# Attention scores in 32-row tiles on a packed key tile, with the exponentials' scale in a register

## The chip, the core and the metric

The kernel runs on one core of one Trainium2 chip. The metric is device time in microseconds, the median of several executions. TensorE (PE) multiplies, VectorE (DVE) reduces and normalises, ScalarE (ACT) computes exponentials and copies, GpSimd (POOL) and SyncE (SP) set things up and issue transfers.

## What is computed

Six sub-layers work on one sequence of 2048 rows of 128 numbers: expert feed-forward, attention, expert feed-forward, ternary feed-forward, attention, ternary feed-forward, each on the layer-normalised rows and added to the residual. The change touches the two attention layers (16 heads of 8 numbers each, causal):

```python
q, k, v = (split_heads(y) for y in (x @ wq, x @ wk, x @ wv))    # 16 heads x 8
scores = where(causal, einsum('bhqd,bhkd->bhqk', q, k), -inf)
attn = softmax(scores / sqrt(8))
x = x + einsum('bhqk,bhkd->bhqd', attn, v) (@ wo + bo in the first)
```

## The kernel before, in words

**Queries and keys as rows.** Each number of q and k is split into float16 parts, so that a head takes TERMS x 8 = 24 rows, plus 8 rows for the negative row maximum (two parts, MAX_UNIT on the key's side) and zeros: 32 rows, a "slot". Four heads (G = 4) make 128 rows, a group g; there are NG = 4 groups. The rows go through DRAM (`slot_dram`) and come back by SP's and POOL's loads (`load_k_rows`, L1084 to L1088, called at L1382 to L1383 and L1397 to L1399; q's at L1394). `q_slots` [128, 4, 2048] holds the four heads of a group together. `k_slots` [128, 16, 2048] holds each head by itself, at its own 32 rows of 128, and zeros in the other 96, so that a matmul over all 128 rows gives one head's scores. POOL writes these zeros once, at the start of the kernel (L620), and then 32 rows of MAX_UNIT (L622); the same tile is the source of the constant rows that SP stores to DRAM at L380 to L385.

**Steps, quads and units.** A step is a pair (g, c) of a group and a chunk c of 512 queries (CH). Steps are taken with c = 0, 1, 2, 3 for g = 0, 1, and then c = 3, 2, 1, 0 for g = 2, 3 (`STEPS`). A step has two kinds of work.

The *units* find the row maximum: for a block of 128 queries, a head and a chunk of 512 keys, PE computes the scores with queries on the partitions (L1204) into one of three PSUM banks, a ring, and DVE reduces them: `tensor_reduce` at L1314, or, on the diagonal, an instruction that also adds the causal mask (L1320). Successive units have successive heads h = 0 to 3. When a step's units are done, DVE makes the negative maximum (L1368), PE turns it (L1209), DVE splits it (L1341, L1343) and SP writes it into `q_slots` (L1410).

The *quads* do the rest, one for each 128 keys j of a step: `score_tile` (L1155 to L1176) computes the scores of two heads, with keys on the partitions, into two banks (L1164), twice; if the quad is on the diagonal (4 quads of each step), a matmul of all 128 rows with `ident_bf` adds the mask to its first 128 columns (L1171). ACT takes the exponentials of each tile of two heads (L1275). `values` (L1178 to L1189) then multiplies them by `v_aug`, four heads in four column groups of 32 (L1184), in float32, which makes eight matmuls a quad. Diagonal quads have 512, 384, 256 and 128 query columns.

**The order.** PE's program is written out turn by turn: score tile 0 of a quad, some ring items, score tile 1, some, the values of the quad before, the rest. `units_beside_quads` gives each turn its number of units, from their columns and from due times (a step's units are done 3 quads before it begins; the first two steps' units run ahead of all quads). A score tile waits for the exponentials of the tile two before it, a unit for its ring bank, the values for their exponentials.

**The scale.** DVE computes one number per layer (`exp_scale`, L818) at the start, and signals `qk_scaled` at L824. The exponentials read it as an operand, a column of SBUF.

The line numbers are those of the profile.

Of the kernel before, what the change touches and what calls it, by code (L numbers as in the profile page):

```python
# [7 lines left out]
F16 = mybir.dt.float16  # L8
I32 = mybir.dt.int32
# [53 lines left out]
def macaron_layers(nc, x_in, wq, wk, wv, wo, bo, wr, w1, b1, wo2, bo2, gamma, beta,  # L63
# [16 lines left out]
    with stack:  # L80
# [15 lines left out]
        q_slots = sb("q_slots", [P, NG, T], F16)  # L96
        k_slots = sb("k_slots", [P, H, T], F16)
        exp_scale = sb("exp_scale", [P, 2])
# [21 lines left out]

        dve_chain = Chain(sem("dve_own"))

        slot_dram = [nc.dram_tensor(f"{n}_rows", [H, TERMS + 1, DH, T], F16, kind="Internal").ap() for n in ("q", "k")]
# [157 lines left out]
        def expert_layer(first, order, given, norms, next_norms, released=None, following=None):  # L281
# [23 lines left out]
            if first:  # L305
# [15 lines left out]
                def staged(cols, rows=P):  # L321
# [25 lines left out]
                    sem("qk_max_ready"), sem("qk_max_turned"), sem("qk_diag_ready"), sem("qk_max_all"))  # L347
                rest_rows_stored, qk_scaled = sem("rest_rows_stored"), sem("qk_scaled")

# [249 lines left out]
            def _(pool):  # L599
                if first:  # L600
# [18 lines left out]

                    pool.memset(k_slots[:, :, :].rearrange("p h t -> p (h t)").bitcast(I32), 0).then_inc(slots_set, 1)  # L620
                    pool.wait_ge(slots_set, 1)
                    pool.memset(k_slots[0:H * MAX_PARTS, 0, :], MAX_UNIT).then_inc(slots_set, 1)  # L622
# [442 lines left out]
        def attention_layer(proj, layer, projected, given, next_norms, next_given, released):  # L1065
# [15 lines left out]

            def load_k_rows(engine, n, h):  # L1084

                cols = slice(n * CH, (n + 1) * CH)
                return engine.dma_start(k_slots[SLOT * h:SLOT * (h + 1), h::G, cols],
                                        slot_dram[1].rearrange("(g h) i d t -> h (i d) g t", h=G)[h, :, :, cols])  # L1088

# [62 lines left out]
            def _(pe):  # L1152
                def score_tile(q, pr):

                    (g, c), j = q  # L1155
                    n = quad_no[q]
                    off = first_query(q)
                    if j == 0 and pr == 0:
                        pe.wait_ge(negmax_landed[step_no[q[0]] % 4], 16 * MAX_PARTS * (step_no[q[0]] // 4 + 1))
                    tile = 2 * n + pr  # L1160
                    if tile >= 2:
                        pe.wait_ge(exp_done, tile - 1)
                    for par in range(2):
                        last = pe.matmul(psum[:, S_BANKS + 2 * (tile % 2) + par, off:CH],  # L1164
                                         k_slots[:, G * g + 2 * pr + par, j * P:(j + 1) * P],
                                         q_slots[:, g, c * CH + off:(c + 1) * CH],
                                         start=True, stop=q not in diagonal)
                    if q in diagonal:

                        for par in range(2):  # L1170
                            last = pe.matmul(psum[:, S_BANKS + 2 * (tile % 2) + par, off:off + P],  # L1171
                                             ident_bf[:, :], later_keys[:, :], start=False, stop=True)
                    last.then_inc(scores_done, 1)
# [16 lines left out]
                def ring_item(item):  # L1190
# [5 lines left out]
                    if kind == "scores":  # L1196
                        (g, c), i, kc, h = what
                        if (g, i, kc, h) == (0, 0, 0, 0):
                            pe.wait_ge(q_landed[c], 16 if c else 16 * (G + 1))
                            if c:  # L1200
                                pe.wait_ge(k_landed[c - 1], 16 * G)
                        w = CH if kc < c else (i + 1) * P
                        qb = BPC * c + i
                        last = pe.matmul(psum[:, bank, 0:w], q_slots[:, g, qb * P:(qb + 1) * P],  # L1204
                                         k_slots[:, G * g + h, kc * CH:kc * CH + w], start=True, stop=True)
                    elif kind == "max":
# [54 lines left out]
            @blk.scalar  # L1261
            def _(act):
                for n in range(1, NCH):
                    proj.high_parts(act, n)
                for (q, _), (_, _, copy_out, _) in zip(TURNS, PLAN):
                    if q:
                        n = quad_no[q]
                        off = first_query(q)
                        for pr in range(2):
                            tile = 2 * n + pr  # L1270
                            act.wait_ge(scores_done, tile + 1)
                            if tile >= NP:
                                act.wait_ge(pv_done, (tile - NP) // 2 + 1)
                            bank = S_BANKS + 2 * (tile % 2)
                            act.activation(probs[:, tile % NP, :, off:CH], psum[:, bank:bank + 2, off:CH],  # L1275
                                           ACT.Exp, scale=exp_scale[:, layer:layer + 1]).then_inc(exp_done, 1)
                    for s in copy_out:
# [94 lines left out]
            @blk.gpsimd  # L1372
            def _(pool):

                for n in range(1, NCH):
                    pool.wait_ge(parts_stored[n % 2], 16 * 2 * TERMS * (n // 2 + 1))
                    for h in range(G):
                        load_k_rows(pool, proj.order[n], h).then_inc(k_landed[proj.order[n] - 1], 16)

            @blk.sync  # L1380
            def _(sp):
                def slots_of(n):  # L1382
# [5 lines left out]
                    for m in range(2):  # L1388
                        sp.wait_ge(proj.lo_ready, 2 * n + m + 1)
                        for i, r in enumerate((Q_PARTS, K_PARTS)[m]):  # L1390
                            sp.dma_start(slot_dram[m][:, i, :, cols],
                                         proj.parts_of(n, m)[:, r, :]).then_inc(parts_stored[n % 2], 16)
                    sp.wait_ge(parts_stored[n % 2], 16 * 2 * TERMS * (n // 2 + 1))
                    sp.dma_start(q_slots[:, :, cols],  # L1394
                                 slot_dram[0].rearrange("(g h) i d t -> (h i d) g t", h=G)[:, :, cols]
                                 ).then_inc(q_landed[c], 16)
                    if n == 0:  # L1397
                        for h in range(G):
                            load_k_rows(sp, c, h).then_inc(q_landed[c], 16)  # L1399

# [55 lines left out]
```

## Time and profile before

| | us |
|---|---|
| median of 3 runs | 1316.02 (1314.12 to 1316.12) |
| span of the profiled execution | 1311.0 |
| PE matmul busy | 1194.1 |
| DVE busy | 1044.4 |
| ACT busy | 723.5 |
| POOL busy | 66.6 |

The profile is of one execution. Its span goes from its first to its last instruction; its own time outside the span is not recorded, and the medians are of other executions of the same program. The first attention layer's quads run from 202.5 to 640.9 us, the second's from 848.5 to 1277.5. Busy time of an engine is the time in which at least one of its instructions was under way; starts of matmuls are recorded, their ends are modelled.

### The profile page before, as it was taken

The page shows a single profiled execution, that of the slowest core. Times are in us where ns is not written, and L with a number is a line of the kernel's source. Part 1 is how long each engine was busy: PE and PEld are TensorE (multiplying, and loading weights), DVE is VectorE, ACT ScalarE, POOL GpSimd, SP SyncE. Part 2 cuts the span into 40 slices and gives each one's busy share as a digit, 9 for nine tenths or more (in the row PEclk, how much of TensorE's full clock was granted, in tenths as well). Part 3 has the DMA queues.
Part 4 walks back from the last instruction along what each step waited for, and adds up shares of the span by engine and source line. Part 5 has one row for each costly group of instructions (what it writes and reads, how often), then busy time and mean ns, then how long its engine had stood idle before and what let it go on. Part 6 is the DMA issues. An engine that isn't in the chain of part 4 may idle for free.

```text
span 1311.0 us, 21446 instructions
## 1 busy us (share of the span) xinstructions
PE 1194.1 (91%) x7781; PEld 510.1 (39%) x7781; DVE 1044.4 (80%) x3015; ACT 723.5 (55%) x861; POOL 66.6 (5%) x64
## 2 busy tenths in 40 slices
PE   1999958999999999999699979599999999999997
PEld 1455533333333333334455537233333333333336
DVE  8976588999999887875447567799999989878764
ACT  1322115566777777777332224156667777777773
POOL 5111010000000000000101000100000000000000
PEclk9999979999999999999799989799999999999999
DMA  4100142000000000000000000510000000000001
GB/s 147 34 1 1 39 131 58 2 1 2 2 1 1 2 1 2 1 1 2 1 0 1 1 1 25 154 48 2 2 1 2 2 1 1 2 1 2 2 2 33
DMA packets 23510, 23.26 MB, mean 18 GB/s; under 512 B 3134, under 2 KB 21220, under 8 KB 23404
## 3 DMA queue, kind: packets, MB, share of 16 engines
q1 hardware_dynamic: 22252, 18.73, 4.9%
q0 software_dynamic: 1152, 3.15, 0.9%
q8 instruction: 62, 1.02, 0.3%
q14 instruction: 44, 0.36, 0.1%
HBM read 13.20 MB, written 8.39 MB: 16 GB/s over the span
## 4 chain that ended last, share of the span: by engine, by line
PE 70%; DVE 22%; issue 4%; ACT 2%; DMA 1%; SPq 0%; DVEq 0%; ACTq 0%
PE psum L1184 18%; PE psum L1204 17%; PE psum L1164 14%; PE psum L442 9%; DVE part_max L1314 8%; PE psum L466 2%; PE psum L903 2%; PE psum L1171 2%; DVE junk L1320 2%; DVE xn L167 1%; DVE norm_v L150 1%; PE psum L1224 1%; PE psum L918 1%; DVE norm_stats L141 1%; PE psum L427 1%
## 5 line engine op out<-in xcount | busy, mean ns | idle before, releaser
L1275 ACT ACTIVATE hidden<-psum,exp_scale 128x1024 f32<-128x1024 f32 (+3 forms) x640 | 597.7, 984 | 258.9 <-PE psum L1164 137.3
L1314 DVE TENSOR_REDUCE part_max<-psum 128x1 f32<-128x512 f32 x768 | 492.1, 686 | 59.1 <-PE psum L1204 53.9
L1204 PE MATMUL psum<-k_slots,q_slots 128*128 128x512 f16 (+3 forms) x1280 | 401.2, 356 | 34.2 <-DVE part_max L1314 12.2
L1164 PE MATMUL psum<-q_slots,k_slots 128*128 128x512 f16 (+3 forms) x1280 | 330.9, 348 | 6.3 <-ACT hidden L1275 3.5
L1184 PE MATMUL psum<-hidden,v_aug 128*9 128x512 f32 (+3 forms) x2560 | 293.7, 531 | 0.1
L1320 DVE CUSTOM_DVE_ANT_0 junk<-psum,causal_add 128x384 bf16<-128x384 f32 (+3 forms) x512 | 230.6, 488 | 49.0 <-PE psum L1204 45.9
L1204 PEld LDWEIGHTS psum<-k_slots,q_slots 128*128 128x128 f16 x1280 | 114.5, 97 | 361.1 <-DVE part_max L1314 177.5
L442 PE MATMUL psum<-parts,w_parts 128*128 128x512 f16 x768 | 180.4, 387 | 1.9 <-DVE parts L843 1.9
L1164 PEld LDWEIGHTS psum<-q_slots,k_slots 128*128 128x128 f16 x1280 | 118.3, 98 | 97.8 <-ACT hidden L1275 13.9
L442 PEld LDWEIGHTS psum<-parts,w_parts 128*128 128x128 f16 x768 | 73.7, 99 | 83.1 <-issue 6.8
L586 ACT CAST parts<-psum 128x512 f16<-128x512 f32 x64 | 37.2, 588 | 107.2 <-PE psum L427 107.2
L1184 PEld LDWEIGHTS psum<-hidden,v_aug 128*9 128x9 f32 x2560 | 38.0, 88 | 91.6 <-issue 81.0
L1171 PE MATMUL psum<-later_keys,ident_bf 128*128 128x128 bf16 x512 | 69.0, 219 | 0.0
L843 DVE TENSOR_TENSOR parts<-parts 128x1024 f16<-128x1024 f16 x64 | 46.8, 755 | 18.2 <-ACT parts L586 18.2
L1171 PEld LDWEIGHTS psum<-later_keys,ident_bf 128*128 128x128 bf16 x512 | 47.5, 98 | 25.2 <-issue 0.7
L1320 DVE DVE_READ_ACCUMULATOR2_ANT part_max<- 128x1 f32 x512 | 42.6, 83 | 0.0
L629 POOL TENSOR_TENSOR x_plus<-xn,bo_bc 128x512 f32<-128x512 f32 x8 | 13.8, 1723 | 568.1 <-DVE xn L167 529.5
L244 ACT COPY xn_t<-psum 128x512 f32<-128x512 f32 x8 | 4.7, 588 | 55.9 <-PE psum L219 55.9
L958 POOL TENSOR_TENSOR x_plus<-x_res,fb_half 128x512 f32<-128x512 f32 x8 | 10.1, 1266 | 494.7 <-DVE xn L167 494.7
L466 PE MATMUL psum<-wo_sb,hidden 128*128 128x128 f32 x256 | 30.1, 276 | 3.7 <-ACT hidden L577 3.7
L946 ACT ACTIVATE hidden<-psum,bias_cols 128x512 f32<-128x512 f32 x32 | 20.0, 688 | 24.3 <-PE psum L918 24.3
L577 ACT ACTIVATE hidden<-psum,unscale 128x512 f32<-128x512 f32 x32 | 19.4, 689 | 23.7 <-PE psum L452 23.7
(170 smaller groups left out, 730.5 us busy)
## 6 DMA issues: line engine op xcount, KB each, us to landing
q_slots<-q_rows SPq DMA_DIRECT2D x8, 512.0 KB, 3.7
k_slots<-k_rows POOLq DMA_DIRECT2D x24, 128.0 KB, 4.1
q_rows<-parts SPq DMA_DIRECT2D x18, 128.0 KB, 2.7
k_rows<-parts SPq DMA_DIRECT2D x18, 128.0 KB, 2.4
q_slots<-in_L_ffn_W_dram SPq DMA_DIRECT2D x2, 1024.0 KB, 6.5
k_slots<-k_rows SPq DMA_DIRECT2D x8, 128.0 KB, 3.9
q_slots<-nm_parts SPq DMA_DIRECT2D x64, 4.0 KB
out_dram<-x_res SPq DMA_DIRECT2D x4, 256.0 KB, 2.3
```

The source lines that it names most:

```text
L442: last = pe.matmul(psum[:, t, :], w1_parts[:, e, wp, t * P:(t + 1) * P], x_mask[:, k % NX, xp, :], start=(e == 0 and (wp, xp) == (0, 0)), ...
L466: last = pe.matmul(psum[:, DOWN_BANK, i * D:(i + 1) * D], hidden[:, n % 2, t, i * P:(i + 1) * P], wo2_sb[:, t, :], start=(t == 0), stop=(t ...
L586: act.copy(mask_sb[:, k % NX, :], psum[:, MASK_BANKS + k % 2, :]).then_inc(mask_ready, 1)
L843: dve.tensor_tensor(x_mask[:, k % NX, :, :], x_parts[:, n % 2, :, :], mask_sb[:, k % NX, :].rearrange("p (a t) -> p a t", a=1).broadcast_t ...
L903: last = pe.matmul(psum[:, 6 + n % 2, i * D:(i + 1) * D], hidden[:, n % 2, t, i * P:(i + 1) * P], tw2_t[:, t, :], start=(t == 0), stop=(t ...
L1164: last = pe.matmul(psum[:, S_BANKS + 2 * (tile % 2) + par, off:CH], k_slots[:, G * g + 2 * pr + par, j * P:(j + 1) * P], q_slots[:, g, c * ...
L1171: last = pe.matmul(psum[:, S_BANKS + 2 * (tile % 2) + par, off:off + P], ident_bf[:, :], later_keys[:, :], start=False, stop=True)
L1184: last = pe.matmul(psum[VW * h:VW * h + DH + 1, O_BANK, off:CH], v_aug[:, j, G * g + h, :], probs[:, (2 * n + h // 2) % NP, h % 2, off:CH] ...
L1204: last = pe.matmul(psum[:, bank, 0:w], q_slots[:, g, qb * P:(qb + 1) * P], k_slots[:, G * g + h, kc * CH:kc * CH + w], start=True, stop=True)
L1275: act.activation(probs[:, tile % NP, :, off:CH], psum[:, bank:bank + 2, off:CH], ACT.Exp, scale=exp_scale[:, layer:layer + 1]).then_inc(ex ...
L1314: dve.tensor_reduce(dst, psum[:, bank, :], axis=AX.X, op=ALU.max).then_inc(ring_read, 1)
L1320: dve.tensor_tensor_reduce(out=junk[:, n % 2, 0:w], in0=psum[:, bank, 0:w], in1=causal_add[:, CH - w:CH], scale=1.0, scalar=-3.0e38, op0=A ...
```

## The change

`k_slots` becomes [128, 4, 2048], laid out as `q_slots`: the four heads of a group share a column range. A score matmul takes only the 32 rows of its head from both tiles (`rows_of`), in the units and in the quads; the mask matmul and the values are as before. The memset of the key tile covers one of the four groups, and the wait between the two memsets goes. Keys are loaded as queries are, by one transfer for a chunk in place of four, and the semaphores' counts follow. Each attention layer's ACT program begins with a wait for `qk_scaled` and a load of the scale into a register, and the exponentials take it from there. The order of the work and the transfers' bytes are the same.

```diff
--- before.py
+++ after.py
@@ -94,7 +94,7 @@
         parts = sb("parts", [P, 8 * 2 * CH], F16)
         x_plus = sb("x_plus", [P, NB, D])
         q_slots = sb("q_slots", [P, NG, T], F16)
-        k_slots = sb("k_slots", [P, H, T], F16)
+        k_slots = sb("k_slots", [P, NG, T], F16)
         exp_scale = sb("exp_scale", [P, 2])
         v_aug = sb("v_aug", [P, NB, H, DH + 1])
         w_qkv0 = sb("w_qkv0", [P, 3, D])
@@ -119,6 +119,7 @@
         fb2_half = sb("fb2_half", [P, D])
 
         dve_chain = Chain(sem("dve_own"))
+        qk_scaled = sem("qk_scaled")
 
         slot_dram = [nc.dram_tensor(f"{n}_rows", [H, TERMS + 1, DH, T], F16, kind="Internal").ap() for n in ("q", "k")]
 
@@ -345,7 +346,7 @@
                 qk_unscale = sb("qk_unscale", [P, 2])
                 qk_max_ready, qk_max_turned, qk_diag_ready, qk_max_all = (
                     sem("qk_max_ready"), sem("qk_max_turned"), sem("qk_diag_ready"), sem("qk_max_all"))
-                rest_rows_stored, qk_scaled = sem("rest_rows_stored"), sem("qk_scaled")
+                rest_rows_stored = sem("rest_rows_stored")
 
 
             if first:
@@ -617,8 +618,7 @@
                     pool.iota(rank[:, :], pattern=[[-1, E]], base=E, channel_multiplier=0,
                               allow_small_or_imprecise_dtypes=True).then_inc(masks_done, 1)
 
-                    pool.memset(k_slots[:, :, :].rearrange("p h t -> p (h t)").bitcast(I32), 0).then_inc(slots_set, 1)
-                    pool.wait_ge(slots_set, 1)
+                    pool.memset(k_slots[:, 1, :].bitcast(I32), 0).then_inc(slots_set, 1)
                     pool.memset(k_slots[0:H * MAX_PARTS, 0, :], MAX_UNIT).then_inc(slots_set, 1)
                     pool.wait_ge(later_loaded, 16 * N_LATER)
                     pool.wait_ge(sums_ready, 2)
@@ -1079,13 +1079,14 @@
             q_landed = [sem(f"q_landed{n}") for n in range(NCH)]
             k_landed = [sem(f"k_landed{n}") for n in range(1, NCH)]
 
-
-
-            def load_k_rows(engine, n, h):
+            def load_rows(engine, slots, m, n):
 
                 cols = slice(n * CH, (n + 1) * CH)
-                return engine.dma_start(k_slots[SLOT * h:SLOT * (h + 1), h::G, cols],
-                                        slot_dram[1].rearrange("(g h) i d t -> h (i d) g t", h=G)[h, :, :, cols])
+                return engine.dma_start(slots[:, :, cols],
+                                        slot_dram[m].rearrange("(g h) i d t -> (h i d) g t", h=G)[:, :, cols])
+
+            def rows_of(h):
+                return slice(SLOT * h, SLOT * (h + 1))
 
 
 
@@ -1161,9 +1162,10 @@
                     if tile >= 2:
                         pe.wait_ge(exp_done, tile - 1)
                     for par in range(2):
+                        rows = rows_of(2 * pr + par)
                         last = pe.matmul(psum[:, S_BANKS + 2 * (tile % 2) + par, off:CH],
-                                         k_slots[:, G * g + 2 * pr + par, j * P:(j + 1) * P],
-                                         q_slots[:, g, c * CH + off:(c + 1) * CH],
+                                         k_slots[rows, g, j * P:(j + 1) * P],
+                                         q_slots[rows, g, c * CH + off:(c + 1) * CH],
                                          start=True, stop=q not in diagonal)
                     if q in diagonal:
 
@@ -1196,13 +1198,13 @@
                     if kind == "scores":
                         (g, c), i, kc, h = what
                         if (g, i, kc, h) == (0, 0, 0, 0):
-                            pe.wait_ge(q_landed[c], 16 if c else 16 * (G + 1))
+                            pe.wait_ge(q_landed[c], 16 if c else 16 * 2)
                             if c:
-                                pe.wait_ge(k_landed[c - 1], 16 * G)
+                                pe.wait_ge(k_landed[c - 1], 16)
                         w = CH if kc < c else (i + 1) * P
                         qb = BPC * c + i
-                        last = pe.matmul(psum[:, bank, 0:w], q_slots[:, g, qb * P:(qb + 1) * P],
-                                         k_slots[:, G * g + h, kc * CH:kc * CH + w], start=True, stop=True)
+                        last = pe.matmul(psum[:, bank, 0:w], q_slots[rows_of(h), g, qb * P:(qb + 1) * P],
+                                         k_slots[rows_of(h), g, kc * CH:kc * CH + w], start=True, stop=True)
                     elif kind == "max":
                         k = step_no[what]
                         pe.wait_ge(negmax_ready, k + 1)
@@ -1260,6 +1262,9 @@
 
             @blk.scalar
             def _(act):
+                scale = act.alloc_register(f"exp_scale{layer}")
+                act.wait_ge(qk_scaled, 1)
+                act.reg_load(scale, exp_scale[0:1, layer:layer + 1].bitcast(I32))
                 for n in range(1, NCH):
                     proj.high_parts(act, n)
                 for (q, _), (_, _, copy_out, _) in zip(TURNS, PLAN):
@@ -1273,7 +1278,7 @@
                                 act.wait_ge(pv_done, (tile - NP) // 2 + 1)
                             bank = S_BANKS + 2 * (tile % 2)
                             act.activation(probs[:, tile % NP, :, off:CH], psum[:, bank:bank + 2, off:CH],
-                                           ACT.Exp, scale=exp_scale[:, layer:layer + 1]).then_inc(exp_done, 1)
+                                           ACT.Exp, scale=scale).then_inc(exp_done, 1)
                     for s in copy_out:
                         k = step_no[s]
                         last_quad = quad_no[(s, BPC * (s[1] + 1) - 1)]
@@ -1374,8 +1379,7 @@
 
                 for n in range(1, NCH):
                     pool.wait_ge(parts_stored[n % 2], 16 * 2 * TERMS * (n // 2 + 1))
-                    for h in range(G):
-                        load_k_rows(pool, proj.order[n], h).then_inc(k_landed[proj.order[n] - 1], 16)
+                    load_rows(pool, k_slots, 1, proj.order[n]).then_inc(k_landed[proj.order[n] - 1], 16)
 
             @blk.sync
             def _(sp):
@@ -1391,12 +1395,9 @@
                             sp.dma_start(slot_dram[m][:, i, :, cols],
                                          proj.parts_of(n, m)[:, r, :]).then_inc(parts_stored[n % 2], 16)
                     sp.wait_ge(parts_stored[n % 2], 16 * 2 * TERMS * (n // 2 + 1))
-                    sp.dma_start(q_slots[:, :, cols],
-                                 slot_dram[0].rearrange("(g h) i d t -> (h i d) g t", h=G)[:, :, cols]
-                                 ).then_inc(q_landed[c], 16)
+                    load_rows(sp, q_slots, 0, c).then_inc(q_landed[c], 16)
                     if n == 0:
-                        for h in range(G):
-                            load_k_rows(sp, c, h).then_inc(q_landed[c], 16)
+                        load_rows(sp, k_slots, 1, c).then_inc(q_landed[c], 16)
 
                 for n in range(NCH - 1):
                     slots_of(n)
```

## Rows read from the trace of the kernel before

**Rows 1.** The page, chain that ended last: shares of the span by engine

```profile
PE 70%; DVE 22%; issue 4%; ACT 2%; DMA 1%; SPq 0%; DVEq 0%; ACTq 0%
```

**Rows 2.** Windows, first attention layer: length; PE, PEld, DVE, ACT, POOL busy; clock; DMA

```profile
202.50:227.60 25.10, 22.53 (x169) 9.69 (x168) 23.23 (x69) 12.42 (x17) 2.18 (x4) 1.00 0.27 74
227.60:277.10 49.50, 46.85 (x316) 17.18 (x315) 46.45 (x124) 29.92 (x34) 0.00 (x0) 1.00 0.01 1
277.10:347.40 70.30, 68.55 (x441) 23.40 (x440) 65.81 (x148) 46.67 (x51) 0.00 (x0) 1.00 0.01 1
347.40:434.20 86.80, 86.50 (x559) 29.16 (x558) 79.23 (x174) 63.52 (x66) 0.00 (x0) 1.00 0.00 1
434.20:518.80 84.60, 83.78 (x549) 27.98 (x547) 72.06 (x168) 63.46 (x66) 0.00 (x0) 1.00 0.01 1
518.80:579.90 61.10, 60.75 (x422) 21.97 (x421) 47.86 (x127) 46.55 (x51) 0.00 (x0) 1.00 0.01 1
579.90:619.50 39.60, 38.20 (x293) 15.37 (x292) 26.58 (x97) 29.51 (x34) 0.00 (x0) 1.00 0.01 2
619.50:640.90 21.40, 16.77 (x153) 8.85 (x151) 12.57 (x60) 12.63 (x19) 4.76 (x4) 0.92 0.00 1
```

**Rows 3.** Timeline 558 to 562, PE: start, length, engine, line, count

```profile
559.39 0.39 PE L1204 MATMUL psum<-k_slots,q_slots 128*128 128x512 f16 x1
...
559.61 1.03 PE L1164 MATMUL psum<-q_slots,k_slots 128*128 128x512 f16 x4
...
560.48 0.38 PE L1204 MATMUL psum<-k_slots,q_slots 128*128 128x512 f16 x1
...
560.78 1.05 PE L1184 MATMUL psum<-hidden,v_aug 128*9 128x512 f32 x8
...
561.76 0.60 PE L1204 MATMUL psum<-k_slots,q_slots 128*128 128x512 f16 x2
```

**Rows 4.** Timeline 0 to 24, POOL and DVE; then the landing of L363's load

```profile
3.00 13.75 POOL L620 MEMSET k_slots<- 128x16384 int32 x1
...
5.13 11.64 DVE L150 TENSOR_SCALAR norm_v<-norm_mean_var 128x4 f32<-128x4 f32 x1
...
16.81 1.82 DVE L152 TENSOR_SCALAR norm_tmp<-norm_v 128x4 int32<-128x4 int32 x1
16.81 1.79 POOL L622 MEMSET k_slots<- 32x2048 f16 x1
...
21.81 2.29 DVE L702 TENSOR_REDUCE wmax<-q_slots 128x1 f32<-128x2048 f32 x1
...
DMA to landing us min/median/max: 7.2/7.2/7.2
```

**Rows 5.** Chain of waits 207 to 215: start, length, engine, line

```profile
213.68 0.11 PE psum L1171 x2
```

**Rows 6.** Timeline 410 to 416, DVE; timeline 558 to 562, ACT

```profile
413.22 3.08 DVE L1314 TENSOR_REDUCE part_max<-psum 128x1 f32<-128x512 f32 x5 [0.42 <-PE psum L1204]
...
560.25 2.12 ACT L1275 ACTIVATE hidden<-psum,exp_scale 128x1024 f32<-128x1024 f32 x2 [0.64 <-PE psum L1164]
```

**Rows 7.** Groups of instructions by shape: count, busy us, mean ns, idle before

```profile
L1184 PE MATMUL psum<-hidden,v_aug 128*9 128x512 f32 x1792 | 234.3, 595 | 0.0
...
L577 ACT ACTIVATE hidden<-psum,unscale 128x512 f32<-128x512 f32 x32 | 19.4, 689 | 23.7 <-PE psum L452 23.7
...
L561 ACT ACTIVATE parts<-psum 128x512 f16<-128x512 f32 x8 | 4.8, 597 | 49.3 <-PE psum L398 49.3
```

**Rows 8.** Timeline 805 to 850, SP's queue; then the chain there

```profile
818.07 0.38 SPq L1394 DMA_DIRECT2D q_slots<-q_rows  x1
818.49 1.93 SPq L1087 DMA_DIRECT2D k_slots<-k_rows  x4
...
819.99 4.13 DMA k_slots<-k_rows
```

**Rows 9.** Windows: a pause of PE before the first exponentials (clock 0.50)

```profile
186.30:191.10 4.80, 0.23 (x3) 0.00 (x0) 4.27 (x24) 0.00 (x0) 2.18 (x4) 0.50 0.76 213
```

## The prediction

> **What bounds the kernel.** I read first the chain of waits, then the busy times by stage, then one turn of the attention engine by engine, then the head of the kernel. A difference of 0.2% (2.6 us) is about what a measurement of this kernel can tell from no change. The profiled execution spans 1311.0 us; the median of the runs is 1316.0, so some 5 us lie around the span, and I take them as constant.
>
> The chain is PE for 70% and DVE for 22% [rows 1]. Where, the stages of the first attention layer show [rows 2], cut at the steps with c = 0 and 1, then 2, 3 and 3, then 2, 1, 0. From 277.1 to 579.9 PE is busy 97 to 100% of each stage, ACT 66 to 76%, and DVE falls from 94% to 78%. Before 277 PE and DVE are both at 90 to 95%. So PE binds, with DVE close behind: DVE's idle time in the stages is 4.9 us (first two together), 4.5, 7.6, 12.5, 13.2 and 13.0. That is the room that a faster PE can win before DVE binds. Stages of the second layer have the same lengths within 2 us, but for its shorter end.
>
> One turn shows what PE does [rows 3]. A full-width matmul starts every 0.22 us: the unit at 559.39 is followed by four scores from 559.61 and the next unit at 560.48, which is 0.87/4. The values (560.78 to 561.76) take 0.98 for eight matmuls of 595 ns each, so they run side by side in the four column groups [rows 7]; and from the unit at 560.48 to the values pass 0.30, so that going over to another shape of tile costs about 0.09. A turn with u units therefore costs 1.07 + 0.86 + 0.22 u. A layer has 160 quads, 96 of them off the diagonal, and 640 units.
>
> **The change, part by part.**
>
> *1. The memset at the head.* POOL clears 128x16384 elements for 13.75 us from 3.00 [rows 4]. DVE's tensor_scalar at L150, on 128x4 elements, begins at 5.13 and lasts 11.64: it ends with the memset, and the one at L152 takes 1.82, until the memset of L622 ends. Both are held by POOL, both are on the chain, and PE and ACT do nothing until the rows that they normalise are there. Now 128x1024 elements are cleared: 1/16, 0.9 us. L622's 1.79 follows at once, so POOL is done at about 5.7, L150 at 5.9, L152 at 6.1 in place of 18.63. Gain 12.5. What is late next: the two reductions at L702, which start at 21.81 and would start at 9.3, the second at 11.6, need both halves of W1; the second is issued at 2.6 and lands 7.2 later, at about 10 [rows 4]. It is there in time. Both ends: 11 us if W1 or a later weight comes late, 12.7 at best. Later weights are wanted tens of us behind that.
>
> *2. The scores of the quads.* Two score matmuls of a tile now use 32 rows each, in different row groups, and write different banks. No row shows row groups at work; the nearest are the column groups of the values [rows 3, 7]. So I take a pair as one, 0.22 for 0.43, which saves 0.43 in each of the 96 quads off the diagonal: 41 us of PE a layer. Bounds: nothing saved (each waits for the other), or the pair fully hidden beside a unit in a third row group (0.86).
>
> The Trainium skill, "TensorE: Matmul & The Clock Gate", section "Measured speedup vs the span model", gives 3.07 times for four 32-row matmuls, not four times. By it a pair would save an estimated 0.15 to 0.2 rather than 0.22, and my gain by attention would be about a tenth less.
>
> *3. The diagonal.* There the mask (L1171) still has 128 rows, between scores that now have 32. Today it costs 0.055 a matmul [rows 5]. Each tile now goes over twice, four times a quad, and by the 0.09 of rows 3 that is 0.36; the scores there, 320 columns wide on average, save 0.27. So the 64 diagonal quads lose 0.1 each, 6 us of PE a layer. Bounds: 0 for the four crossings, or 0.8.
>
> *4. The units (L1204).* Successive units have successive heads, so row groups differ and banks do too. They overlap only where the ring of three banks is free, that is where DVE isn't behind. I take a quarter of their time, 20 to 30 us of PE a layer; bounds none and two thirds.
>
> *5. What DVE lets through.* A reduction comes every 0.60 us in a run of five [rows 6], and DVE's work is unchanged. So stage by stage the gain is the smaller of PE's relief and DVE's idle time, less something for unevenness between turns. Relief: 8, 16, 24, 24, 16 and 8 quads off the diagonal at 0.43 make 3.5, 7, 10, 10, 7, 3.5; the diagonal takes back 1.6 and then 0.8 each; the units give 6, 5, 7, 6, 3.5, 1. Together 8, 11, 17, 16, 10, 4, against DVE's idle time of 4.9, 4.5, 7.6, 12.5, 13.2, 13.0 [rows 2]. I take 3, 4, 7.5, 11.5, 9, 3: **38 us a layer, 76 in both**. The stage of c = 0 at the end waits on the chain through DVE's normalisation and gains nothing. Bounds: 29 a layer if units don't overlap at all, half of that if little is collected; 56, all of DVE's idle time, at best.
>
> *6. The exponentials.* An ACTIVATE of 128x512 with a pointer operand takes 689 ns, one without 597 [rows 7], so the register should save some 0.09 of each of 640, if it works as an immediate does; else nothing. Two in a row take 2.12 [rows 6], so ACT needs about 2.0 a turn where PE takes 2.4 or more: ACT is hidden today. With turns at 2.1 it would be nearly exposed, and the 0.18 a turn keeps it covered. I count no gain of its own. If the saving fails, the stages after 518 give back 3 us a layer. The wait and register load at the head of each layer's ACT program have no row; ACT waits for PE's transposes there, so I count 0 (bounds 0 and 1 us each).
>
> *7. The key loads.* At the head of a layer SP issues q's load at 818.07 and then four key loads in 1.93; the last lands 4.13 after 819.99, and the first units wait for it [rows 8]. One load of the same 512 KB is issued right behind q's, so it lands about 1.1 us earlier, on the chain: 2.2 for both layers. SP's later row stores move up 1.5 with it. POOL's 24 issues become 6 where POOL is idle: nothing.
>
> **Sum.** 1316.0 - 12.5 - 76 - 2.2 = 1225; I say 1226.
>
> **Rivals.**
> *A. The overlap comes, but little is collected.* PE's order is fixed: units, scores and values wait for ring banks and exponentials in turn, so a PE with slack may just wait elsewhere. For it: before 277 both engines are busy to 90 or 95% and still neither is full. Against: three ring banks hold 1.8 us of DVE's work, more than the values' 1.07. A third to two thirds of the 76: 1250 to 1276. Chance 0.15.
>
> *B. 32-row matmuls do not overlap, and the crossings are paid* (the change would not do what it says). PE then keeps its 0.86 for scores and pays 0.36 in each diagonal quad, some 50 of 64 a layer uncovered: 36 us for both layers, against 14.7 gained by parts 1 and 7: 1337. It decides from 0.15 us a quad on. Against it: the column groups of the same engine overlap now. Chance 0.04.
>
> The Trainium skill, "TensorEngine Tiling (Array Packing)", section "Key Properties", says that changing the tiling mode drains the engine. The 0.09 before the values agrees with that.
>
> *C. TensorE's clock falls.* Today it is granted in full (2.4 GHz) in every stage of rows 2 but the last (0.92); it was at half, 1.2 GHz, in 186.3 to 191.1, where PE was busy 0.23 of 4.8 us [rows 9]. With a quarter of the rows at work and PE waiting for DVE, the clock may be granted less. At 1.2 GHz a turn off the diagonal would cost PE about 3.9 (values 1.9, pairs 0.86, units 1.1) where it would cost 2.1 at full clock: if this holds for half of the 192 such turns, 96 x 1.8 = 173, and 1226 + 173 = 1399. It turns the gain of 91 into a loss once a quarter of the turns are so. Against: the values use few columns of the array now, and the clock stays full; PE would still be 85% busy. Chance 0.08.
>
> **How the numbers follow.** Forecast 0.73, A 0.15, B 0.04, C 0.08. The forecast's own bounds are 1200 (56 a layer less unevenness) and 1243 (no overlap of units); the range 1200 to 1273 takes in most of A. Faster 0.87, within 0.2% 0.02, slower 0.11.
>
> **What would show it.** L150 at 0.2 to 0.8 us and L702 starting at 9 to 10; pairs of L1164 starting well under 0.22 apart; 0.1 us before and behind L1171; DVE at over 93% busy from 277 to 520, PE below 90%; turns off the diagonal of 2.3 us around 350 to 520 and 2.1 around 550; L1275 at 1.02 for 1024 columns; the clock at 1.00 between the heads. The forecast is wrong if L1164's pairs stay 0.22 apart, if the clock shows 0.5 within a layer, or if DVE is idle as much as now while PE waits for it.

## The result, and the profile after

The changed kernel takes **1362.0 us** (median; 1357.9 to 1387.3) against 1315.9 before: ratio 1.035, interval 1.033 to 1.037. It is slower by 46 us; forecast were 1226 us and a range up to 1273. The ratio leaves out the one execution of 1387.3, whose mean clock was lower (0.817, the others 0.839 to 0.849). The profiled execution took 1361.5, its span is 1359.3 (before 1311.0).

The page of the kernel after: PE's busy time and share, the granted clock in 40 slices, the chain's shares.

```profile
PE 1213.3 (89%) x7781; PEld 417.2 (31%) x7781; DVE 1024.7 (75%) x3015; ACT 671.1 (49%) x861; POOL 45.1 (3%) x46
...
PEclk9999855555699996999799979555895899999999
...
PE 61%; DVE 28%; issue 6%; ACT 3%; DMA 1%; SPq 0%; DVEq 0%; ACTq 0%
```

The same row of the kernel before:

```profile
PEclk9999979999999999999799989799999999999999
```

The kernel before has full clock in nearly every slice; after, it is half for a stretch of each attention layer. The mean granted clock is 0.842 against 0.975. With levels 1 and 0.5 that is 2 x (0.158 x 1359 - 0.025 x 1311), so 364 us more at 1.2 GHz.

The windows of the kernel after, cut at the same steps as [rows 2] (length; PE, PEld, DVE, ACT, POOL busy; clock; DMA):

```profile
194.60:228.40 33.80, 32.03 (x172) 7.62 (x171) 23.89 (x69) 11.75 (x17) 0.75 (x1) 0.53 0.18 55
228.40:298.40 70.00, 67.50 (x318) 12.79 (x315) 48.00 (x124) 27.98 (x35) 0.00 (x0) 0.50 0.01 1
298.40:383.90 85.50, 80.51 (x440) 15.61 (x439) 65.60 (x148) 43.01 (x51) 0.00 (x0) 0.64 0.00 1
383.90:466.50 82.60, 75.03 (x558) 18.57 (x557) 77.35 (x175) 57.96 (x67) 0.00 (x0) 0.98 0.01 1
466.50:552.60 86.10, 79.53 (x548) 17.80 (x547) 70.25 (x169) 57.69 (x66) 0.00 (x0) 0.84 0.01 1
552.60:608.20 55.60, 51.24 (x421) 13.90 (x419) 46.27 (x126) 42.08 (x50) 0.00 (x0) 1.00 0.01 1
608.20:645.90 37.70, 34.88 (x293) 11.12 (x291) 26.27 (x97) 26.92 (x35) 0.00 (x0) 1.00 0.01 2
645.90:667.80 21.90, 18.44 (x153) 6.85 (x151) 13.33 (x60) 11.57 (x19) 4.97 (x4) 0.84 0.00 1
```

Stage by stage against [rows 2]: +8.7, +20.5, +15.2, -4.2, +1.5, -5.5, -1.9, +0.5. Where the clock is at 0.50 to 0.53, PE is 95 to 96% busy and the stage is 35 to 41% longer; where it is at 0.98 to 1.00, the stage is shorter. By steps, the first five (c = 0, 1 and the first with c = 2) lose 43.6 us: they take 17.6, 16.2, 37.1, 32.9 and 51.3 for 13.3, 11.8, 26.2, 23.3 and 36.7.

The balance over the span: quads begin 7.9 us earlier (194.6 for 202.5), the first layer's quads take 34.8 more (473.2 for 438.4), the second's 19.1, and the work between the layers 2.2, though the key load gives 0.6 there; 0.1 is behind them. That is the 48.3 by which the span grew.

### The profile page after: what moved, and what is told of

It is laid out like the page before. It is cut to its first block, busy times and chain, and to the rows that moved or that the text cites. A ratio compares the mean times of both kernels' runs of the same rounds, so it can differ in the third digit from the quotient of the medians.

```text
span 1359.3 us, 21424 instructions
## 1 busy us (share of the span) xinstructions
PE 1213.3 (89%) x7781; PEld 417.2 (31%) x7781; DVE 1024.7 (75%) x3015; ACT 671.1 (49%) x861; POOL 45.1 (3%) x46
## 4 chain that ended last, share of the span: by engine, by line
PE 61%; DVE 28%; issue 6%; ACT 3%; DMA 1%; SPq 0%; DVEq 0%; ACTq 0%
PE psum L1186 18%; DVE part_max L1319 17%; PE psum L1206 14%; PE psum L443 9%; PE psum L1166 5%; PE psum L1173 4%; PE psum L467 2%; DVE junk L1325 2%; PE psum L1226 2%; PE psum L903 2%; ACT hidden L1280 1%; PE psum L918 1%; DVE xn L168 1%; PE psum L428 1%; PE psum L229 1%
## 5 line engine op out<-in xcount | busy, mean ns | idle before, releaser
L1280 ACT ACTIVATE hidden<-psum 128x1024 f32<-128x1024 f32 (+3 forms) x640 | 544.0, 896 | 364.7 <-PE psum L1173 189.4
L1206 PE MATMUL psum<-k_slots,q_slots 32*128 32x512 f16 (+3 forms) x1280 | 408.0, 413 | 73.0 <-DVE part_max L1319 39.8
L1186 PE MATMUL psum<-hidden,v_aug 128*9 128x512 f32 (+3 forms) x2560 | 349.4, 623 | 0.1
L1206 PEld LDWEIGHTS psum<-k_slots,q_slots 32*128 32x128 f16 x1280 | 96.7, 94 | 513.0 <-DVE part_max L1319 286.4
L1166 PE MATMUL psum<-q_slots,k_slots 32*128 32x512 f16 (+3 forms) x1280 | 244.8, 398 | 9.5 <-ACT hidden L1280 7.5
L1173 PE MATMUL psum<-later_keys,ident_bf 128*128 128x128 bf16 x512 | 80.9, 246 | 0.0
L1166 PEld LDWEIGHTS psum<-q_slots,k_slots 32*128 32x128 f16 x1280 | 55.1, 94 | 51.1 <-ACT hidden L1280 25.4
L1173 PEld LDWEIGHTS psum<-later_keys,ident_bf 128*128 128x128 bf16 x512 | 30.2, 100 | 70.1 <-issue 63.8
L467 PEld LDWEIGHTS psum<-wo_sb,hidden 128*128 128x128 f32 x256 | 32.9, 210 | 5.6 <-ACT hidden L578 4.7
L680 DVE TENSOR_TENSOR x_plus<-psum,x_plus 128x512 f32<-128x512 f32 x8 | 5.5, 691 | 35.4 <-PE psum L467 35.4
```

What stands on the lines that cost most here:

```text
L467: last = pe.matmul(psum[:, DOWN_BANK, i * D:(i + 1) * D], hidden[:, n % 2, t, i * P:(i + 1) * P], wo2_sb[:, t, :], start=(t == 0), stop=(t ...
L1186: last = pe.matmul(psum[VW * h:VW * h + DH + 1, O_BANK, off:CH], v_aug[:, j, G * g + h, :], probs[:, (2 * n + h // 2) % NP, h % 2, off:CH] ...
L1206: last = pe.matmul(psum[:, bank, 0:w], q_slots[rows_of(h), g, qb * P:(qb + 1) * P], k_slots[rows_of(h), g, kc * CH:kc * CH + w], start=Tru ...
```

## The experiments

All ratios are to the kernel before, on the same chip. Steps are cut at their first exponential. "Thin" is a unit or score matmul on 32 rows, "full" one on 128; a "crossing" is the change from one tile shape to another.

### Which part costs the time

First the head alone: half of one group's zeros at the start, the rest in 14 pieces between POOL's later work. All matmuls have 128 rows.

```diff
-  pool.memset(k_slots[:, :, :].rearrange("p h t -> p (h t)").bitcast(I32), 0)
+  pool.memset(k_slots[:, 0:2, :].rearrange("p h t -> p (h t)").bitcast(I32), 0)
...
+  if first:                         # once per chunk n, behind POOL's additions
+      for h in range(2 + 4 * n, min(H, 6 + 4 * n)):
+          pool.memset(k_slots[:, h, :].bitcast(I32), 0)
```

> The kernel before, with only the memset at the head cut into pieces (two heads first, the others behind POOL's work on each chunk). Key tile, 128-row matmuls, pointer scale and four key loads as before. All theories: the two held DVE instructions at the head go, 12.5 us less, 1303 us, clock 0.97 or over. If the head's gain is lost later, 1314 to 1316.

1311.1, ratio 0.998 (0.996 to 0.999), clock 0.966, between the two outcomes named; the attention steps are as before. L150 takes 1.8. The first expert's mask multiply comes 11.7 us earlier (20.8 for 32.5), but the third chunk's only 3.0 (90.4 for 93.4; in the changed kernel 80.9). So 8.7 are lost again between 45 and 90 us, where the pieces lie.

On this base, 32 rows in the score matmuls: in both kinds, in the units only, in the quads only. Key tile, four key loads and pointer scale are those of before.

```diff
-  q_slots[:, g, ...],  k_slots[:, G * g + h, ...]
+  q_slots[rows_of(h), g, ...],  k_slots[rows_of(h), G * g + h, ...]
```

> As h_rows128, but units and quads take 32 rows of the zero-padded key tile. Theory 1 (the 32-row matmuls alone bring the lower clock): as the changed kernel within 10 us, 1355 to 1370, clock about 0.84. Theory 2 (the packed tile, the register or the single key load is behind it): at most 1303, clock 0.97. Theory 3 (crossings between tile shapes cost the time, the clock is a by-product): 1340 or more, with turns on the diagonal longer also where the clock is full.

> As h_rows128, with 32 rows in the units only. If the granted clock goes by how many rows are at work: it falls in the first stages, where most units are, 1315 to 1340. If it goes by the time in which PE is busy: units seldom overlap since they wait for DVE, so the clock stays and the time is 1295 to 1303.

> As h_rows128, with 32 rows in the quads' scores only. If the clock goes by busy time: pairs overlap and PE's busy time falls by 0.43 us a turn, so it falls as in the changed kernel, 1340 to 1360. If by rows at work: three kinds of matmul of which one has 32 rows, a fall in the first stages only, 1290 to 1320.

| 32 rows in | median | ratio (95%) | mean clock |
|---|---|---|---|
| units and quads | 1371.1 | 1.044 (1.042 to 1.045) | 0.841 |
| units only | 1371.4 | 1.043 (1.040 to 1.046) | 0.950 |
| quads only | 1325.0 | 1.009 (1.007 to 1.010) | 0.959 |
| none (first run) | 1311.1 | 0.998 (0.996 to 0.999) | 0.966 |

Both together: the first five steps of the first layer are those of the changed kernel, to 0.1 us and with the same clock (0.55 in the first, then 0.50); in the second layer the low stretches fall in part on other steps. So the 32-row matmuls by themselves do it; packed tile, register and single load are not needed. Here and in the first run the key tile is the same, with zeros in the other 96 rows. The full matmuls multiply these zeros and have the full clock, so it is not the useful products that make the difference.

The next two rows fell outside both of their expectations. With thin units alone the six steps with some low clock (the first three of each layer) lose 17 us together; the other steps, at full clock, lose 36, up to 2.9 each, which I read as crossings. With thin and full matmuls in turn all through them, the clock of these steps is 1.00; so crossings alone do not lower it. Timeline of "units only", PE (start, length, engine, line, count):

```profile
419.32 0.39 PE L1211 MATMUL psum<-k_slots,q_slots 32*128 32x256 f16 x2
419.64 0.60 PE L1171 MATMUL psum<-q_slots,k_slots 128*128 128x512 f16 x2
420.18 0.39 PE L1211 MATMUL psum<-k_slots,q_slots 32*128 32x512 f16 x1
420.49 0.61 PE L1171 MATMUL psum<-q_slots,k_slots 128*128 128x512 f16 x2
```

The thin unit at 420.18 is followed by the next matmul only at 420.49, 0.31 later, where neighbours of one shape are 0.22 apart. Each thin unit between full scores pays about 0.1 on either side. "Quads only" shows the overlap:

```profile
445.79 0.39 PE L1211 MATMUL psum<-k_slots,q_slots 128*128 128x512 f16 x1
446.11 0.39 PE L1171 MATMUL psum<-q_slots,k_slots 32*128 32x512 f16 x2
446.43 0.60 PE L1211 MATMUL psum<-k_slots,q_slots 128*128 128x512 f16 x2
```

The two scores at 446.11 start 3 ns apart in the trace and pass in 0.32 with the crossing behind them, in place of 0.43; the crossing ahead of them (445.79 to 446.11 is 0.32, not 0.22) takes the gain back.

### What the clock goes by

My argument against a lower clock was that PE would stay busy. The next run takes every head's scores from rows 0 to 31 (it computes each group's first head four times): as few rows at work, but score matmuls cannot overlap, so PE is busier.

```diff
 def rows_of(h):
-    return slice(SLOT * h, SLOT * (h + 1))
+    return slice(0, SLOT)
```

> The changed kernel, with every unit and score matmul on rows 0 to 31: all heads of a group are computed as its first one. No matmul lies beside another, so PE is busy as long as before the change, with a quarter of the rows. Theory 1 (the clock goes by the rows at work): it falls in the first stages as in the changed kernel or more, 1370 or over, mean clock 0.84 or less. Theory 2 (it goes by the time in which PE is busy; overlapping made PE idle): the clock stays over 0.95 and the time is 1300 to 1335, the crossings at the diagonal and to the values included.

Four executions took 1823.9 to 1955.9 us (before 1314.6), with mean clocks of 0.676 to 0.625; the profile is of the fastest. Windows of its first attention layer, columns as above:

```profile
196.00:321.00 125.00, 123.61 (x485) 31.48 (x484) 73.88 (x192) 40.41 (x51) 0.75 (x1) 0.53 0.05 16
321.00:535.00 214.00, 213.87 (x720) 48.90 (x719) 111.66 (x237) 75.92 (x83) 0.00 (x0) 0.50 0.00 1
```

PE is busy 213.9 of 214.0 us, and the clock stays at half: the steps (0, 2), (1, 2) and (0, 3) take 214.3 us for 114.1. **Busy time alone does not hold the clock.** The opposite test slows DVE, with 128 rows in every matmul and the zeros placed as in the kernel under "Keeping the gains":

```diff
 if kc < s[1]:
+    own.wait()
+    own(dve.memset(spare[:, :], 0.0))
     dve.tensor_reduce(dst, psum[:, bank, :], axis=AX.X,
```

> As late_zeros (128 rows), with a memset of 128x256 elements on DVE ahead of each full-width reduction, 384 a layer, so that PE waits for DVE. Nothing of the computation is changed. Theory 1 (the clock goes by the rows at work): PE is busy to 85 to 92% of the stages up to c = 3, as in the changed kernel at full clock or less, and the clock stays at 1.00 there; 1299 plus DVE's added time, 1350 to 1400. Theory 2 (busy time): the clock falls to 0.50 in the first stages, 1430 or over.

1405.6, ratio 1.069 (1.067 to 1.071); of the two theories it is the first, with 6 us more than its 1400. Windows of its first layer:

```profile
194.60:277.00 82.40, 69.36 (x440) 25.60 (x438) 78.01 (x245) 36.58 (x47) 2.18 (x4) 0.98 0.09 24
277.00:360.00 83.00, 74.16 (x441) 23.14 (x440) 79.77 (x233) 42.83 (x50) 0.00 (x0) 1.00 0.01 1
```

PE is busy only 84% and 89% of these, less than in the slow stages of the changed kernel (95 to 96%), and the clock is 0.98 and 1.00. So a PE that waits for DVE keeps its clock here, as long as its matmuls have all rows.

The next run has more of the thin matmuls: each unit is issued twice.

```diff
+  for _ in range(2):
       last = pe.matmul(psum[:, bank, 0:w], q_slots[rows_of(h), g, ...], ...)
```

> The changed kernel, with every unit matmul issued twice into the same bank, which fills time in which PE waits for DVE. Theory 1 (rows at work): 32 rows more for 0.22 us each, the clock rises somewhat, 1330 to 1360. Theory 2 (busy time): PE is busy as before the change, the clock stays at 1.00 in the first stages and the time is 1270 to 1300. If neither holds and the extra matmuls only cost: 1380 or over.

1489.7, ratio 1.133 (1.128 to 1.137): neither theory, but the third outcome named, that the extra matmuls only cost. Three windows of its first layer:

```profile
200.00:300.00 100.00, 97.17 (x521) 21.68 (x517) 62.66 (x162) 34.56 (x44) 0.75 (x1) 0.57 0.05 15
300.00:400.00 100.00, 94.59 (x621) 21.73 (x619) 72.66 (x166) 46.31 (x56) 0.00 (x0) 0.80 0.01 1
400.00:500.00 100.00, 90.94 (x714) 22.57 (x710) 81.17 (x184) 60.74 (x70) 0.00 (x0) 0.95 0.01 2
```

The mean clock (0.849) is hardly above 0.842: more thin work costs its time, and the time at 1.2 GHz does not shrink (452 us, 431 in the changed kernel).

Between 32 and 128 rows: 64 rows in all unit and score matmuls, on the tile with a head's own rows and zeros beside them.

```diff
-  return slice(SLOT * h, SLOT * (h + 1))
+  return slice(2 * SLOT * (h // 2), 2 * SLOT * (h // 2 + 1))
```

> As late_zeros, with every unit and score matmul on 64 rows: heads 0 and 1 of a group on rows 0 to 63, heads 2 and 3 on 64 to 127 (zeros beside each head). The two scores of a tile share their rows and so do not overlap; neighbouring units do at times. If the clock goes by the rows at work: between 128 rows (mean clock 0.972) and 32 rows (0.84), with 0.50 in part of the early stages, 1310 to 1360. If only 32-row matmuls bring it down: clock 0.96 or over and 1295 to 1315, crossings included.

1336.6, ratio 1.018 (1.015 to 1.021), mean clock 0.932, as the first expectation has it. Its windows where the changed kernel has 0.50 to 0.53:

```profile
194.00:230.00 36.00, 32.40 (x197) 9.94 (x196) 29.43 (x86) 15.88 (x22) 2.18 (x4) 0.86 0.19 52
230.00:300.00 70.00, 65.56 (x377) 17.11 (x376) 55.94 (x142) 33.31 (x40) 0.00 (x0) 0.83 0.00 1
```

With 32, 64 and 128 rows these stages have 0.50 to 0.53, 0.83 to 0.86, and 1.00. The records hold only the two levels, 1.00 and 0.50; a value between is a mean over stretches at either.

### The scale from a register

The changed kernel with the pointer operand back.

```diff
-  ACT.Exp, scale=scale)
+  ACT.Exp, scale=exp_scale[:, layer:layer + 1])
```

> The changed kernel with the scale as a pointer operand again. The exponentials are 88 to 92 ns longer each. If ACT stays covered: 1362 within 4 us. If ACT is exposed once PE has slack: 5 to 15 us more, in the steps behind c = 3.

1372.0, ratio 1.042 (1.037 to 1.046), which just touches that of the changed kernel. Steps at full clock in both show what the scale is worth there: (1, 3) and (2, 3) are alike, and from (3, 3) on the pointer costs 0.2 to 0.7 us a step ((2, 2) takes 28.16 for 27.61 and 26.77 for 26.07), some 2 us a layer. The kernel with 32 rows in units and quads, which has the pointer too, has the same longer steps. That makes 4 of the 10 us between the medians. The rest goes with the stretches at 0.50, which lie on different steps in the two profiles.

Per instruction the register does what an immediate does: 596 ns for 512 columns, where one without a pointer took 597 [rows 7]. The groups of 1024 columns, after and then before:

```profile
L1280 ACT ACTIVATE hidden<-psum 128x1024 f32<-128x1024 f32 x448 | 434.1, 1023 | 223.3 <-PE psum L1166 173.6 <-PE psum L1173 48.7
```

```profile
L1275 ACT ACTIVATE hidden<-psum,exp_scale 128x1024 f32<-128x1024 f32 x448 | 475.8, 1113 | 173.4 <-PE psum L1164 137.3 <-PE psum L1171 35.7
```

It is 90 ns less each, and nearly all of it becomes waiting: between the first run of this section and the next kernel below, both with full rows, all exponentials together take 57.3 us less (597.7, 540.4) and ACT idles 53.9 more before them (258.3, 312.2).

### Keeping the gains

Full rows, register scale, and the zeros of the later heads placed one per expert of the last chunk.

```diff
+  if first:
+      for h in range(2, H):
+          pool.wait_ge(mask_ready, 16 + h)
+          pool.memset(k_slots[:, h, :].bitcast(I32), 0)
```

> The kernel before with 128 rows throughout, the scale from a register, and the zeros of the key tile written one head at a time, one for each expert of the last chunk of the first layer. If the pieces cost little there: the head's 12.5 us are kept, 1303. If a lower clock before the first attention layer takes part of it: 1306 to 1311, as with the earlier pieces.

1299.2, ratio 0.989 (0.987 to 0.991), clock 0.972: 15.4 us, more than either expectation. Some 3 I put to the shorter exponentials (the last steps of each layer are 0.1 to 0.9 shorter, the others unchanged but for one, 0.3). The rest I put to the head, but the profile, taken of the longest execution (1303.6), does not show 12.5: its first mask multiply comes 11.7 earlier, the fourth chunk's 9.6 (117.2 for 126.8), and quads begin 7.8 earlier. The same zeros in the first run above kept only 3.8, without the register. Less the register's 3, some 8 us are their place.

On this base, thin rows in steps 8 to 14 only, where the changed kernel gains; then the same without the diagonal turns.

```diff
+  THIN = range(7, 14)
...
+  thin[0] = q is not None and step_no[q[0]] in THIN
```

> As late_zeros, with 32-row units and scores in the turns of steps 8 to 14 of 16 only, where the changed kernel ran mostly at full clock and gained 0.7 to 3.7 us a step over the kernel before. If the clock holds there: 17 us a layer less than late_zeros, about 1270. If it falls once 32 rows are used at all, wherever: 1300 to 1320, with the clock at 0.50 in stretches of these steps.

> As thin_from_7 (1288 us), but the diagonal quads' turns keep 128 rows. If the crossings round the diagonal mask cost about 0.1 each, four a quad, and the full-row turns help to hold the clock: 3 to 8 us less, 1280 to 1285. If DVE binds in these turns anyway and the clock drops come from the turns off the diagonal: 1286 to 1290.

1287.8 (0.981; 0.978 to 0.984; clock 0.951), between its two expectations, and 1289.4 (0.980; 0.978 to 0.982; 0.941). No difference can be told; stretches at 0.50 remain in both (37.5 us in one step of the second). So a step that ran at full clock in one kernel need not do so in another. Last, thin turns between full ones, in steps 3 to 14: every other quad off the diagonal, or two of three.

```diff
+  thin[0] = ... and q not in diagonal and q[1] % 2 == 0    # every other
+  thin[0] = ... and q not in diagonal and q[1] % 3 != 2    # two of three
```

> As thin_off_diagonal, but over steps 3 to 14, and only in every other quad. If the clock goes by rows averaged over several turns: it stays at 1.00 everywhere, half of the gain off the diagonal is kept, 1280 to 1288. If any 32-row turn can bring it down: stretches at 0.50 in the steps with c = 1 and 2, 1300 or over.

> As thin_every_other (1283.5 us), but two of three off-diagonal quads of steps 3 to 14 have 32 rows. If the clock has room left: a third more of the gain, 1276 to 1281. If it falls once most turns are thin: stretches at 0.50 and 1285 to 1310.

**1283.5, ratio 0.976 (0.975 to 0.977)**, and 1307.9, ratio 0.995 (0.994 to 0.997). The clock rows of the two, in this order, and then three windows of the first layer of "every other":

```profile
PEclk9999979999999999999799979799999999999998
```

```profile
PEclk9999988899999989999799979788889999999998
```

```profile
191.50:334.40 142.90, 133.55 (x925) 45.50 (x923) 134.50 (x339) 80.83 (x102) 2.18 (x4) 1.00 0.05 14
334.40:500.80 166.40, 161.04 (x1106) 47.53 (x1104) 150.28 (x342) 115.48 (x132) 0.00 (x0) 1.00 0.01 1
500.80:598.10 97.30, 93.81 (x711) 32.69 (x710) 73.89 (x223) 68.87 (x84) 0.00 (x0) 1.00 0.01 2
```

Every other turn thin keeps 1.00 in these steps (in the second layer but for one stretch of 3.4 us) and beats both kernels, by 32 us against before. Half of that, 16 us, is gained on the kernel with full rows and late zeros (1299.2); the thin turns bring no more than this. Two of three brings the short stretches at 0.50 back (3 to 10 us in several steps) and gives 24 of these away.

## Why the prediction was wrong, point by point

**Rival C came true; the step that failed is its weighing,** and with it the sum, which priced every turn at full clock. C's sentence "the values use few columns of the array now, and the clock stays full; PE would still be 85% busy" took PE's busy time as what holds the clock, and one row of an idle PE [rows 9] as the only road to 0.50. Measured, PE 95 to 100% busy with 32-row scores is at 0.50 to 0.53, and PE 84% busy with 128 rows at 0.98. Few columns with all rows (the values) do not tell what few rows do. I gave it 0.08.

The Trainium skill, "TensorE: Matmul & The Clock Gate", section "Part 1: The HAM clock gate (the "warmup" mystery)", says that the monitor sets the clock by how busy PE has been. The trace disagrees: with all scores on rows 0 to 31 PE is 99.9% busy at 0.50. The measurement decides: the same order of work with 128 rows has 1.00 in these stages.

C's prices were fair, its arithmetic incomplete. A turn at 1.2 GHz was put at 3.9 us; (0, 2) takes 51.3 for 12 quads, 4.3 each with its diagonal (3.06 before). C counted turns off the diagonal alone, but the steps with c = 0 and 1, whose quads are half or all on the diagonal, lose 29.0 of the 43.6.

**Part 1** (the head, 12.5) held, and is not all kept. Timeline of the head after; then the chain there:

```profile
3.00 0.95 POOL L621 MEMSET k_slots<- 128x1024 int32 x1
...
3.89 1.79 POOL L622 MEMSET k_slots<- 32x2048 f16 x1
...
4.91 0.80 DVE L151 TENSOR_SCALAR norm_v<-norm_mean_var 128x4 f32<-128x4 f32 x1
5.75 0.17 DVE L153 TENSOR_SCALAR norm_tmp<-norm_v 128x4 int32<-128x4 int32 x1
```

```profile
2.61 8.84 DMA q_slots<-in_L_ffn_W_dram
11.44 0.02 issue
11.47 2.29 DVE wmax L702
```

L153 is done at 5.9, against 18.6 for L152 in [rows 4]. W1's second half is next late, as named; it lands at 11.5, not 10. The first expert's mask multiply comes 12.5 earlier (20.0 for 32.5), the fourth chunk's 12.6 (114.2 for 126.8). But quads begin only 7.9 earlier. Ahead of them the clock is low:

```profile
172.60:193.10 20.50, 13.53 (x36) 5.54 (x35) 15.49 (x70) 2.76 (x4) 0.75 (x1) 0.50 0.26 92
```

This is not shown to be the thin units' doing: with full rows there and the later zeros, quads begin at 191.5 to 194.7 in six kernels, and the changed kernel with a pointer scale, whose units ahead are as thin, begins at 192.3. The spread of 3 us belongs to the single execution as far as is known.

The Trainium skill, "SBUF — State Buffer", section "SBUF: two separate sides", says that VectorE and GpSimd can share a port pair that one of them holds for its whole instruction. The trace agrees: L150 ends with the memset in [rows 4], and after (L151) it ends at 5.71, as the short one ends at 5.68.

**Parts 2 and 4** (pairs and units overlap) held where the clock is full. PE in one turn of the changed kernel:

```profile
446.20 0.38 PE L1206 MATMUL psum<-k_slots,q_slots 32*128 32x512 f16 x1
446.23 0.57 PE L1166 MATMUL psum<-q_slots,k_slots 32*128 32x512 f16 x4
447.17 0.38 PE L1206 MATMUL psum<-k_slots,q_slots 32*128 32x512 f16 x1 [0.38 <-DVE part_max L1319]
447.77 0.38 PE L1206 MATMUL psum<-k_slots,q_slots 32*128 32x512 f16 x1 [0.21 <-DVE part_max L1319]
448.08 1.05 PE L1186 MATMUL psum<-hidden,v_aug 128*9 128x512 f32 x8
```

From the first start to the last end a unit and four scores take 0.60, where they took 1.25 in [rows 3] (559.39 to 560.64). Then PE waits for DVE: 0.38 and 0.21.

**Part 3** (0.09 a crossing) held to 0.01:

```profile
456.46 0.60 PE L1166 MATMUL psum<-q_slots,k_slots 32*128 32x512 f16 x2
456.99 0.28 PE L1173 MATMUL psum<-later_keys,ident_bf 128*128 128x128 bf16 x2
457.21 0.38 PE L1206 MATMUL psum<-k_slots,q_slots 32*128 32x512 f16 x1
```

The two masks take 0.22 with the crossing behind them, where two at [rows 5]'s 0.055 would take 0.11. Over the trace the median distance between starts is 151 ns, not 55, behind a 128-column matmul, and 316, not 216, behind one of 512.

**Part 5** was mis-sized, so rival A holds where C does not. From the steps that ran at full clock in either layer (the first with c = 3 at 0.96), the last four stages with a forecast gain 4.3, 7.1, 5.8 and 2.2 us, where 7.5, 11.5, 9 and 3 were forecast: 19.4 of 31. The first two stages never ran at full clock, so their 7 stay untested. With 23 us less in both layers and 1 less in part 7 the forecast would have been 1250, an estimate, and inside its range; what took the time out of the range is the clock. In the step (1, 3), at full clock and 2.5 us shorter:

```profile
426.00:466.50 40.50, 36.90 (x278) 9.31 (x278) 38.07 (x87) 28.97 (x34) 0.00 (x0) 1.00 0.00 1
```

DVE is at 94% and PE at 91%. That the rest goes because PE takes its work in order (units held up behind the values, then DVE idle) is read from such turns and was not tried.

**Part 6**: right, 90 ns each; what it feared without the saving, 3 us a layer in the late stages, is some 2. **Part 7**: 0.6 us a layer, not 1.1. The chain at the head of the second layer:

```profile
845.35 5.00 DMA k_slots<-k_rows
850.35 0.14 issue
```

The one load is issued 1.5 us sooner behind q's than the last of four, but takes 5.00 where that took 4.13 [rows 8].

## What to carry to other kernels

A change that cuts matmuls to a quarter of the rows should be priced at half clock too, before its overlap is counted. Look at the granted clock stage by stage, and try thin turns between full ones where it falls; here that kept the clock. Keep shapes together within a turn: each crossing costs 0.1 us here, so a pair of crossings takes back what one overlapped pair of scores gains (0.2). A long memset on POOL can stand in the way of tiny DVE instructions, so its place is worth as much as its length.

## What the runs showed of the hardware that I had not expected

- With the same order of work the clock of the early stages was 0.50 with 32-row score matmuls (PE 96% busy, and 99.9% where none overlapped), 0.83 with 64 rows, and 1.00 with 128 (89% busy where DVE was slowed). What exactly it goes by stays open.
- In the changed kernel it is low mostly in steps of few keys, and full in (1, 3) in both layers, with the same 32-row matmuls. It is not always low in the same ones: (1, 1) is at 0.50 throughout in the first layer, for 9 of 24 us in the second, and (3, 3), with many keys, has a mean of 0.75 in the first and 1.00 in the second.
- Thin units alone cost 60 us against the same kernel with full rows (1371.4 for 1311.1), 36 of it in steps at full clock, where turns as the one shown lose 0.1 us at each crossing.
